# A decoder layer's softmax sums, query norm and split tiles dealt out anew among ACT, DVE and POOL

## The reference, cut to what matters

```python
kv = concatenate([context, latents], axis=1)            # 1857 rows of 512
q = rms_norm((latents @ Wq).heads(32), q_norm_w)        # head size 128
k = rms_norm((kv @ Wk).heads(8), k_norm_w); v = (kv @ Wv).heads(8)
probs = softmax(q @ k.T / sqrt(128))                    # 4 query heads share a key head
out = (probs @ v).reshape(...) @ Wo
```

## Time and profile before

| | us |
|---|---|
| median of 3 runs | 2817.41 (2812.55 to 2819.07) |
| the profiled execution | 2816.99 |
| its span in the trace | 2815.2 |
| PE busy | 2720.3 (97%) |
| POOL busy | 2377.3 (84%) |
| DVE busy | 2221.7 (79%) |
| ACT busy | 2029.4 (72%) |

### The profile page before, as it was taken

One profiled execution on the slowest core, in us unless ns is written; L12 is line 12 of the kernel. 1 busy time (PEld: TensorE's weight loads), 2 busy tenths in 40 slices (PEclk: granted clock), 3 DMA queues, 4 the chain that ended last, 5 costly groups with the idle time before them and its releaser, 6 DMA issues.

```text
span 2815.2 us, 47816 instructions
## 1 busy us (share of the span) xinstructions
PE 2720.3 (97%) x14812; PEld 2220.4 (79%) x14812; DVE 2221.7 (79%) x3596; ACT 2029.4 (72%) x3945; POOL 2377.3 (84%) x2320
## 2 busy tenths in 40 slices
PE   7899999999999999999999999999999999999974
PEld 5777878777878888888888888888888888888853
DVE  5577888888778878888778887787778888788873
ACT  3577777777767777777777777777777777777771
POOL 4399999898888888878889988888898888888893
PEclk9999999999999999999999999999999999999996
DMA  6756565565555454555545455554455445344310
GB/s 234 253 184 216 193 221 193 195 213 184 183 178 200 160 177 169 182 177 196 178 147 193 167 189 174 179 184 165 156 173 173 154 158 180 124 165 150 117 42 26
DMA packets 159434, 485.64 MB, mean 173 GB/s; under 512 B 16839, under 2 KB 27849, under 8 KB 159182
## 3 DMA queue, kind: packets, MB, share of 16 engines
q1 hardware_dynamic: 157592, 481.01, 50.5%
q10 hardware_dynamic: 1590, 1.58, 0.2%
HBM read 403.09 MB, written 79.43 MB: 171 GB/s over the span
## 4 chain that ended last, share of the span: by engine, by line
PE 79%; POOL 9%; issue 6%; DVE 4%; ACT 2%; DMA 1%; SPq 0%; POOLq 0%; ACTq 0%; DVEq 0%
PE K_ps L971 9%; PE K_ps L973 9%; PE K_ps L972 9%; PE OT_ps L1001 7%; PE S_ps L971 6%; PE S_ps L973 6%; PE S_ps L972 6%; POOL acc L906 5%; PE OT_ps L971 5%; PE OT_ps L972 4%; PE OT_ps L973 4%; POOL P_lo L888 2%; PE F_ps L971 2%; PE F_ps L972 2%; PE F_ps L973 2%
## 5 line engine op out<-in xcount | busy, mean ns | idle before, releaser
L906 POOL TENSOR_TENSOR acc<-acc,scores 128x512 f32<-128x512 f32 (+1 forms) x832 | 1120.8, 1347 | 40.4 <-ACT scores L1323 10.1
L888 POOL TENSOR_TENSOR P_lo<-scores,P_hi 128x512 fp32r<-128x512 f32 x672 | 898.4, 1337 | 211.3 <-ACT scores L1323 210.3
L1652 DVE SCALAR_TENSOR_TENSOR running_max<-S_ps,rk,running_max 128x512 f32<-128x512 f32 (+1 forms) x896 | 669.0, 747 | 250.2 <-ACT scores L1309 247.8
L1636 DVE TENSOR_TENSOR scores<-scores,Mb_ps 128x512 f32<-128x512 f32 (+1 forms) x960 | 648.7, 676 | 134.4 <-PE Mb_ps L1127 134.3
L1309 ACT ACTIVATE scores<-S_ps,rk 128x512 f32<-128x512 f32 (+1 forms) x960 | 651.6, 679 | 139.8 <-PE S_ps L973 120.1
L1323 ACT ACTIVATE scores<-scores 128x512 f32<-128x512 f32 (+1 forms) x960 | 596.9, 622 | 59.2 <-DVE scores L1636 57.1
L1322 ACT ACTIVATE P_hi<-scores 128x512 fp32r<-128x512 f32 x672 | 423.1, 630 | 293.7 <-DVE scores L1636 213.9
L971 PE MATMUL S_ps<-QT_hi,KT_hi 128*128 128x512 f32 (+1 forms) x960 | 496.9, 518 | 14.8 <-DVE running_max L1652 13.0
L971 PE MATMUL K_ps<-Wkv_hi,kvT 128*128 128x256 f32 (+1 forms) x1664 | 470.9, 283 | 2.4 <-DVE kvT L1709 2.4
L973 PE MATMUL K_ps<-Wkv_hi,kvT 128*128 128x256 f32 (+1 forms) x1664 | 471.1, 283 | 0.0
L972 PE MATMUL K_ps<-Wkv_lo,kvT 128*128 128x256 f32 (+1 forms) x1664 | 470.3, 283 | 0.0
(11 more groups left out here) (226 smaller groups left out, 4666.8 us busy)
## 6 DMA issues: line engine op xcount, KB each, us to landing
kvT<-kvT_scratch SPq DMA_DIRECT2D x403, 512.0 KB, 3.7
Wq_hi<-weight_halves_scratch SPq DMA_DIRECT2D x48, 512.0 KB, 5.4
Wq_lo<-weight_halves_scratch SPq DMA_DIRECT2D x48, 512.0 KB, 6.6
Wo_hi<-weight_halves_scratch SPq DMA_DIRECT2D x48, 512.0 KB, 4.7
Wo_lo<-weight_halves_scratch SPq DMA_DIRECT2D x48, 512.0 KB, 5.6
kvT_scratch<-built SPq DMA_DIRECT2D x45, 512.0 KB, 4.3
rinv_spread<-rinv_scratch SPq DMA_DIRECT2D x64, 256.0 KB, 4.8
Wkv_hi<-weight_halves_scratch SPq DMA_DIRECT2D x24, 512.0 KB, 5.6
```

Of the source, the lines that this page charges most:

```text
L888: e.tensor_tensor(P_lo[n % PB][0:r, :], prob(t)[0:r, :], f(P_hi[n % PB][0:r, :]), ALU.subtract)\
L906: e.tensor_tensor(a[0:r, :], a[0:r, :], prob(t)[0:r, :], ALU.add).then_inc(s_acc, 1)
L1636: e.tensor_tensor(d, d, Mb_ps[0:r, :], ALU.add).then_inc(s_d, 1)
L1652: e.scalar_tensor_tensor(a, src, k, a, ALU.mult, ALU.max).then_inc(s_top, 1)
```

## The change

- `FULL` goes from 7, 5, 3, 3 tiles of 15 to 5, 3, 1, 1, and to other places. Two more tiles of every half are split: 128 of 960.
- Of every half the tiles 2, 7 and 11 are no longer added by POOL. DVE reduces each by a `tensor_reduce` that transposes in blocks of 32 x 32 (`sum_tile`, one step after the exponential). In the two halves of the last unit (`LATE`) all 15 tiles go this way and POOL adds none. ACT zeroes the last tile's unused rows there.
- Instead of AT's four transpositions DVE reduces `acc` in the same way and adds up the blocks, one step before AT (`sum_blocks`). AT is now one small fp32 matmul (16 weight columns, 32 columns) with `same`; DVE takes the reciprocal from PSUM straight into `rrow`. RT is gone: store and spread follow AT in 1 and 3 steps instead of 3 and 5, the division in 7 instead of 8.
- `normalise` moves from DVE (two instructions) to ACT (eight of 128 columns, four each at c = 13 and 14).
- `EVENTS` lie at tiles 2, 7, 11 of every half. `built` has one buffer instead of two.

```diff
-    FULL = [[2, 3, 6, 7, 10, 11, 14], [4, 5, 10, 11, 14], [6, 7, 14], [6, 7, 14]]
+    FULL = [[0, 1, 12, 13, 14], [12, 13, 14], [14], [14]]
+    SUMMED = [[2, 7, 11]] * B
+    LIGHT = [[2, 7, 11]] * B
     FULL = [FULL[v // KVH] for v in range(UNITS)]
+    SUMMED = [SUMMED[v // KVH] for v in range(UNITS - 1)] + [list(range(NJ))]
+    ADDED = [NJ * p + j for p in range(HALVES) for j in range(1, NJ) if j not in SUMMED[p // 2]]
+    LATE = [p for p in range(HALVES) if len(SUMMED[p // 2]) == NJ]
...
-            12: [("RT", 2 * v - 3)],
...
-            27: [("RT", 2 * v - 2), ("QT", v, 1)],
+            27: [("QT", v, 1)],
...
     def divided(s):
-        return [x[1] for x in fill(s - 6) if x[0] == "RT"]
+        return [x[1] for x in fill(s - 7) if x[0] == "AT"]
...
-        if j in FULL[p // 2] and j - 1 not in FULL[p // 2] and j < NJ - 1:
+        if j in LIGHT[p // 2]:
             EVENTS.append(s)
...
             def store_reciprocals(p):
-                e.wait_ge(s_fr, F_AT["RT", p] + 1)
+                e.wait_ge(s_fr, F_AT["AT", p] + 1)
...
                 for x in fill(s - 1):
-                    if x[0] == "RT":
+                    if x[0] == "AT":
                         store_reciprocals(x[1])
...
             def add(t):
                 p, j = divmod(t, NJ)
-                if j == 0:
+                if t not in ADD_AT:
                     return
...
-            def turn_sums(p):
-                e.wait_ge(s_acc, acc_no(NJ * p + NJ - 1))
+            def add_blocks(p):
...
+                e.wait_ge(s_bt, p + 1)
                 out = take(("AT", p))
-                for i in range(4):
-                    ins = e.transpose(out[:, i * P:(i + 1) * P], acc[p % 2][:, i * P:(i + 1) * P], ident[:])
...
+                e.matmul(out[0:16, 0:32], sums[:, p % 2, :], same[:], start=True, stop=True).then_inc(s_ff, 1)
...
+                if r < P and p in LATE:
+                    e.activation(row[s % RING][TAIL // 32 * 32:P, :], row[s % RING][TAIL // 32 * 32:P, :], ACT.Copy,
+                                 scale=0.0).then_inc(s_z, 1)
...
+            def normalise(v, t):
+                e.wait_ge(s_nw, 5 * RT_AT["q", v] + 5)
+                e.wait_ge(s_kr, K_AT["Q", v, t] + 1)
+                for h in range(GR):
+                    ins = e.activation(natq[t][:, h, :], natq[t][:, h, :], ACT.Copy, scale=rq[:, 4 * t + h:4 * t + h + 1])
+                ins.then_inc(s_nat, 1)
...
+            def sum_tile(t):
+                p, j = divmod(t, NJ)
+                e.wait_ge(s_p, t + 1)
+                e.tensor_reduce(blocks_of(p)[:, SUMMED[p // 2].index(j), :], prob(t).rearrange("p (j a) -> p j a", a=32), AX.X,
+                                ALU.add, apply_transpose=True).then_inc(s_bs, 1)
+
+            def sum_blocks(p):
...
+                    e.wait_ge(s_acc, ADD_AT[NJ * p + NJ - 1] + 1)
+                    e.tensor_reduce(blocks_of(p)[:, n, :], acc[p % 2][:].rearrange("p (j a) -> p j a", a=32), AX.X,
+                                    ALU.add, apply_transpose=True).then_inc(s_bs, 1)
...
+                e.reduce_sum(sums[:, p % 2, :], blocks_of(p)[:, 0:n + 1, :].rearrange("p k j -> p j k"), AX.X)\
+                    .then_inc(s_bt, 1)
...
-                for kind, v in rooted(s - 4):
-                    if kind == "q":
-                        normalise(v)
+                if 0 <= s - WAIT - 1 < NS and summed_tile(s - WAIT - 1):
+                    sum_tile(s - WAIT - 1)
+                for x in fill(s + 1):
+                    if x[0] == "AT":
+                        sum_blocks(x[1])
```

More of the change, by code:

```diff
@@ L312, in left @@
         return NJ * (2 * v - 3) + max(kind[v - 2][at]) + 1 if kind[v - 2][at] else 0
+    BLOCKS = []
+    for s in STEPS:
+        if 0 <= s - WAIT - 1 < NS and summed_tile(s - WAIT - 1):
+            BLOCKS.append(s - WAIT - 1)
+        BLOCKS += [("acc", x[1]) for x in fill(s + 1) if x[0] == "AT" and x[1] not in LATE]
+    BLOCK_AT = {x: n for n, x in enumerate(BLOCKS)}
     with ExitStack() as ctx:
@@ L400, in layer @@
         xrow = sb("xrow", [P, E])
-        built = [sb(f"built{i}", [P, 2, C, P], F32R) for i in range(2)]
+        built = sb("built", [P, 2, C, P], F32R)
         ident = sb("ident", [P, P])
@@ L703, in store_tile @@
                 k = x_no(b, n)
-                src = tile[k % 3] if b == 0 else built[k % 2]
+                src = tile[k % 3] if b == 0 else built
                 e.wait_ge(s_fr, F_AT["X", b, n] + 1)
@@ L1471, in _ @@
                     copy_scores(s)
+                for t in range(TPB):
+                    for kind, v in rooted(s - 4 - t):
+                        if kind == "q":
+                            normalise(v, t)
                 for x in fill(s):
@@ L1706, in drain @@
                         k = x_no(b, n)
-                        to = tile[k % 3] if b == 0 else built[k % 2]
+                        to = tile[k % 3] if b == 0 else built
                         hi, dst = to[:, 0, :, 0:r], to[:, 1, :, 0:r]
```

91 lines of the change are left out of this document (50 added, 41 removed).

## The result

The changed kernel takes 2834.58 us (median; 2832.82 to 2841.47), the kernel before 2816.67 us beside it: ratio 1.0066, 95% interval 1.0054 to 1.0078. It is 18 us slower; the forecast was 2763 us, 54 us faster. The profiled execution of the changed kernel has a span of 2834.4 us, 19.2 longer than the span before.

A forecast was written before the change was run, and what follows sets the result against it. PE was taken to set the pace over 60 halves, POOL in the last three. PE -39, ACT +3 and the end -18 make -54 us: span 2761, time 2763 us (chance 0.70), range 2738 to 2796.

The forecast's parts named there:

- The end: Last three halves and what follows: -3.4, -1, -11 and 2.5 us off the tail, -18 us in all (-3 to -22).
- The reduction: DVE's transposing reduction costs as much as the plain one, 0.68 us; sign in the trace: 0.65 to 0.75 us.
- the small matmul: On PE, replacing AT's and RT's transpositions: two instructions at 0.24 us, saving 0.31 us a half over 60 halves.
- The engines' sums over a unit: Busy time per unit of 80 us after the change: DVE some 67 us, about 83%, and ACT 68.
- The norm on ACT: Eight norm pieces, 2.8 us a unit, at c = 13 and 14; all ACT's added work was charged +3 us (0 to +16).
- PE's idle time in batches 1 and 2: Sign in the trace: PE idle under 4 us from 850 to 2199 us.
- a unit takes 80.8 us: Sign in the trace: a mid-run unit of 80.1 us instead of 81.4; wrong if it stays at 81.
- two more split tiles at -20 us: On PE, two tiles a half go from 0.86 to 0.69 us: 0.34 us a half over 60 halves.
- what is taken from PE is taken from the time, until another engine is later: From a mid-run half whose PE work sums to its 41.0 us: PE has no wait, so its savings shorten the time.
- "ACT late": Rival: ACT can't run ahead of PE, 1 us a unit lost from c = 14 to 20: +27, 2790 us; chance 0.07.

## Why the forecast was wrong

**What held.** The end gained 17.6 us against 18. Its parts were off by 1 to 2 us each and made up for one another: by the forecast's steps -3.4, -1 and -11 for the last three halves and -2.5 behind them, measured -1.5, 0, -11.4 and -4.7. The reduction takes 0.69 us (0.65 to 0.75 said), the small matmul 0.17 (0.24 said). The engines' sums over a unit held as well: DVE has 65.4 us of 80.8 (67 of 80 said), ACT 67.3 (68 said). The norm on ACT gave 3 us in the one pair of kernels that shows it, where the forecast charged ACT 3. Of the signs that it named, two didn't come: PE's idle time in batches 1 and 2 is 12.9 us and not under 4, and a unit takes 80.8 us and not 80.1.

**A term too large: the small matmul at 0.31 us a half.** It saved 0.2. Where PE stands idle in no record, in batch 2, the two halves of a unit took 41.0 and 40.4 us before, and with the small matmul, but with the old list and the old places (the fastest kernel), 40.8 and 40.1. First the kernel before, then the fastest one:

```profile
1916.14:1956.53 40.39, 40.39 (x228) 33.90 (x227) 30.11 (x51) 32.09 (x62) 36.34 (x37) 1.00 0.44 159
```

```profile
1865.75:1906.57 40.82, 40.82 (x230) 34.31 (x229) 32.39 (x54) 33.29 (x70) 31.30 (x34) 1.00 0.57 192
1906.57:1946.71 40.14, 40.14 (x225) 33.42 (x224) 32.91 (x54) 31.98 (x63) 32.35 (x34) 1.00 0.48 160
```

Over 60 halves that is some 12 us instead of 19. With the end's 17.6 it makes the 30 us that the fastest kernel gained (2787.07 against 2817), where the forecast's steps for all of the change but the list give 19 and 18 less 3 for ACT, 34.

**The step that failed: two more split tiles at -20 us.** They cost 31 us (with the pieces at their new places; 65 with the old). PE did have less to do; the step "what is taken from PE is taken from the time, until another engine is later" failed in its second half. The forecast compared the engines' sums per unit, and DVE and ACT had 12 to 13 us free of 80. The first batch has no such room: at steps 13 to 20 the weights of Wo are split on ACT and POOL as well, and PE waited there already. Three experiments divide the 31 us. Some 20 are the places of the unsplit tiles in the first batch (2834.58 against 2814.84), the half clock among them. Number may count too: in the fastest kernel two more split tiles in the first batch alone cost 12.5. The three buffers of the halves cost some 3 us in the first batch (705.2 against 701.9). How much of the rest falls on ACT's exponentials and how much on POOL's subtractions was not taken apart; the kernel without the reductions (2904 us, POOL at 656 of 740) shows that POOL's are dear. In batches 1 to 3 the list neither gains nor loses much (batches 1 and 2 take 1349.8 us with it and 1345.6 without), and that is a miss as well: some 15 of the 20 us were forecast for their 44 halves. Against the same unit with the old list, 40.8 and 40.1 us, the changed kernel has 40.96 and 39.84: one half gains 0.3 us, as forecast, and the other loses 0.1. So a unit takes 80.8 us, where 80.1 was forecast and 81.4 stood before. In the half that loses, PE's recorded busy time hides a wait for the maximum ahead of its transposition:

```profile
1936.98 0.28 PE L994 MATMUL K_ps<-Wkv_hi,kvT 128*128 128x256 f32 x1
1937.39 0.66 PE L1139 MATMUL F_ps<-ident,running_max 128*128 128x128 f32 x4
```

Matmuls like the first one are 0.12 us apart; here the next instruction starts after 0.41. By that maximum's start, 1936.59, DVE had waited 0.22 us for ACT's copy of the scores, which tells part of the delay.

**The step that was missing: the self-attention pieces.** The change moved `EVENTS` to tiles 2, 7 and 11. The text described this ahead of the prediction, and the sum had no term for it. With the old list it costs 16 us, and one place alone costs 15; with the new list it saves 18. The forecast had costed what each engine has to do, and a piece that is only moved has no cost in such a ledger.

**"ACT late" came in part.** The rival gave 2790 us for 1 us a unit lost at c = 14 to 20. The place was right. The engine was ACT in some of the waits: six of PE's thirteen waits for the maximum in the first batch take 0.8 us each, and before each DVE stood idle for ACT's copy of the scores, as here:

```profile
687.45 0.75 DVE L1688 SCALAR_TENSOR_TENSOR running_max<-S_ps,rk,running_max 128x512 f32<-128x512 f32 x1 [0.97 <-ACT scores L1330]
...
688.26 0.50 PE L992 MATMUL S_ps<-QT_hi,KT_hi 128*128 128x512 f32 x1 [0.79 <-DVE running_max L1688]
```

The norm has little part in it, since moving it back to DVE changes nothing. But four waits of 4.6, 4.1, 2.8 and 2.0 us make 13.5 of the 20.1, and before each of them DVE had instructions that lasted long beside POOL: three times those of a self-attention piece, once a division. The price was too low also because of what such a wait does next. The dearest one, in the changed kernel on DVE, POOL and PE:

```profile
417.22 4.50 DVE L1616 TENSOR_TENSOR self_small<-self_small 128x256 f32<-128x256 f32 x1
...
416.62 2.38 POOL L966 TENSOR_TENSOR Wo_lo<-w_stage,Wo_hi 128x1024 fp32r<-128x1024 f32 x1
418.96 1.25 POOL L909 TENSOR_TENSOR P_lo<-scores,P_hi 128x512 fp32r<-128x512 f32 x1
420.18 1.25 POOL L927 TENSOR_TENSOR acc<-acc,scores 128x512 f32<-128x512 f32 x1
...
423.03 0.80 PE L992 MATMUL S_ps<-QT_hi,KT_hi 128*128 128x512 f32 x1 [4.59 <-DVE running_max L1688]
```

A subtraction that takes 0.42 us in the fastest kernel (at 398.48 there) lasts 4.50, until after POOL's third instruction has ended at 421.43. PE stands for 4.6 us, and then runs slower. The stretch after the wait (granted clock in the third column from the right):

```profile
423.03:427.04 4.01, 4.01 (x15) 3.73 (x16) 3.55 (x6) 3.45 (x7) 3.46 (x3) 0.50 0.55 223
```

Up to the wait PE had full clock; in the 4.0 us after it PE has half, 1.2 GHz, so that some 2 us more are lost. A wait of 4.6 us costs some 6.6.

**Still open.** Why the old places are the worse ones with the new list was seen (2852 against 2835 us), and explained only in part. In the kernel with the new list and the old places the longest DVE instructions of the first batch are two divisions of 4.45 and 4.18 us (at 245.47 and 605.23), each beside POOL's work and each followed by a wait of PE for the maximum of 2.6 us; the changed kernel has one such. What moves them there was not tested. Nor do experiments divide PE's 13.3 us of waits for POOL's subtraction. Before the longest of them, 2.1 us at 516.1, POOL had worked without a pause since its split of Wo at 507.20, so there it was POOL itself that was late. The opening is 4 to 6 us longer in some kernels (178.6 us in the changed one, 171.9 to 180.2 in all); no run isolates that.

## What to carry to other kernels

An engine with 15% of its time free may still have none where it counts. Before work is moved to it, add up the few steps in which the bound engine waits for it already, not the unit. And give every moved instruction a term, also one that is only moved by a step: ask what the other engine is doing at the new place. A busy time of 100% does not show that an engine waits for nothing: look at the starts, and at the granted clock of the stretch, before you call a loss idle time or work. When a change has several parts, run them as a table of two by two: here the fastest kernel is most of the change (the sums, the norm, the end) without its list and without its new places, 47 us faster than the whole.

## What the runs showed of the hardware

- A DVE instruction with operands in SBUF that takes 0.15 us beside an idle POOL took 1.2 to 1.6 us beside a busy one, and one of 0.42 us took 4.50. The Trainium skill, page "SBUF — State Buffer", section "Who interferes with whom", says that DVE and GpSimd share a port pair, that a DVE instruction with two SBUF inputs contends with a GpSimd one that reads SBUF, and that who issues first blocks the other for the whole instruction. The three small instructions bear this out: each ends with the POOL instruction that it met. The one of 4.50 us doesn't: POOL's instruction that it met ended at 419.00, and the DVE instruction was still under way through two more, until after 421.43. The division of 4.18 us at 605.23 in the kernel with the new list and the old places does the same: POOL's instruction that it met ended at 606.36, and the division lasted through two more, until after 608.85. The size of a DVE instruction is no protection: single columns were held as well.
- A transposing reduction of 128 x 512 takes 0.69 us, as much as a plain one, and was not held up by POOL: all 186 reductions of tiles before the last unit lie between 0.685 and 0.706 us.
- After a wait of 4.6 us PE's granted clock was 0.50 for 4.0 us. The first batch of the changed kernel has 20.5 us at 0.50, that of the kernel before none.
